# One-hots with nodes on partitions: compared from repeated rows of relative numbers in place of transposed, in the attention and the gate stage

## The chip, the cores and the metric

The kernel runs on one core of one Trainium2 chip. The metric is the device time of one execution in microseconds (us). Median before: 5861.45 us over 3 runs (5858.7 to 5862.68).

## What is computed

A graph network of four layers on 6250 nodes with 128 features and 100000 edges `(src, dst)`, sorted by `dst`. Each layer has a LayerNorm and a ReLU ahead of it and adds to `x`. Cut to what matters here:

```python
x = x + L0(h)                     # APPNP: two rounds of a normalised neighbour sum, then two dense layers
# L1, attention:
q, k, v = nodes @ Wq + bq, nodes @ Wk + bk, nodes @ Wv + bv
e = edge_attr_128 @ We
alpha = sum_per_head(q[dst] * (k[src] + e)) / sqrt(16)
attn = softmax of alpha over the edges of each dst
out = segment_sum(attn * (v[src] + e), dst)
x = x + L2(h)                     # two rounds of a neighbour mean, dense layers
# L3, gates:
xr, xc = h[src], h[dst]
gates = softmax(concat(x_src, x_dst, x_edge) @ W_gate + b_gate)   # three gates for each edge
out = segment_sum(gates[0] * x_src + gates[1] * x_dst + gates[2] * x_edge, dst)
```

## The kernel before, in words

Edges lie in tiles of 128, and nodes in 49 blocks of 128. A *step* is one tile of edges against one block of nodes (a tile that spans two blocks gives two steps): 832 steps. Four steps (`U = 4`) are a *part*, four parts (`PARTS = 4`) a turn; there are 208 parts. Buffers of a part are used in a ring of four, by `r = n % 4`; some PSUM banks and staging buffers in a ring of two (`RING2`). All order is written by hand: each engine runs its own list of steps, `edge_loop` and `stretch_loop` call the steps of an engine with a lag in parts, and semaphores join them.

`rel_col` holds, for each step and each edge on its partition, the edge's node relative to its block. A one-hot with **edges on partitions** is `iota == rel`, and is the weight of the product that adds messages to nodes (`hot`, `hot_sum`). A one-hot with **nodes on partitions** is needed to fetch a value of the destination node for each edge (`q[dst]` in the attention, the destination's logits in the gate stage) by a product with the block's rows. Before the change it is `hot` transposed: TensorE transposes, ScalarE copies PSUM to `hot_t`.

**Attention stage** (L1150 to L1470). Part `n` on each engine:
- GpSimd (`att_pool`, L1228): four indirect gathers of rows of `tab_kv` into `rows`, each followed by `weigh_part` (L1213), which multiplies the values of a part 39 parts back by their weights, or, as long as there is none, by a memset that paces the gathers (L1235). It may start part `n` once part `n - 4` is scored (`kv_done`).
- SyncE (`att_sp`): `att_load` (L1154), four loads of edge attributes for part `n`; `value_store` (L1171) of part `n - 3`, after its `kv_done`; `value_load` (L1166) of part `n - 37`, after the sums of four parts earlier (`win_done`). These stand in this order in one queue.
- VectorE (`att_dve`): `make_hot(n)` (L1417), then `score_part(n - 2)` (L1432, L1435, L1439, L1444), with the adds of summed messages (L1404) between.
- TensorE (`att_pe`): `turn(n)` transposes attributes (L1331) and `hot` (L1333); `products(n - 1)` gives `e` (L1344) and `q[dst]` (L1346); `sums` (L1357) of part `n - 40`.
- ScalarE: copies both transposes (L1275, L1276), weights and one-hots of the sums (L1248, L1253, L1258).

The 208 parts are cut into seven stretches; at the end of each, a chain for the softmax's maxima runs on VectorE, TensorE and ScalarE (`max_dve`, `max_pe`, `max_act`), and VectorE scores nothing meanwhile.

**Gate stage** (L1711 to L1800). GpSimd (`gathers`, L381) gathers rows of `tab_gate`, each gather followed by a memset (L384); part `n` waits for `gate_msg` of part `n - 4`. VectorE runs, for each part: `logits(n - 2)` (L1758 to L1763, waits for the gathered rows), `message(n - 3)` (L1781), `gates(n - 2)` (L1769 to L1773), `step_hot(n)` (L390), adds of part `n - 4` (L455). TensorE runs `logits(n - 1)` (L1743), `sums(n - 3)` (L432) and `turn(n)`, the transposes (L1732); ScalarE copies them (L1711), and does `exp` and `scale` (L1705, L1716). SyncE has nothing to do in this stage.

`d_reset` is a table in DRAM of one row of 128 for each step, written once in the set-up (L1915).

## Time and profile before

| | |
|---|---|
| median of 3 runs | 5861.45 us |
| the profiled execution | 5857.49 us, its span 5855.7 us |
| busy: PE, DVE, ACT, POOL | 68%, 51%, 24%, 59% of the span |
| attention stage, gathers from 1821.0 to 3200.1 us | about 1380 us |
| gate stage, gathers from 4590.3 to 5792.7 us | about 1204 us |
| granted TensorE clock over the span | 0.79 |
| DMA queue of SyncE (q1) | 611.37 MB, 32.6% of 16 engines |
| DMA queue of GpSimd (q0) | 224.30 MB, 14.1% of 16 engines |

PE is TensorE, PEld its weight loads, DVE VectorE, ACT ScalarE, POOL GpSimd, SPq the queue of SyncE, which issues most DMAs. "L381" is line 381 of the kernel. A busy share of the whole span mixes stages that have different limits, so stages are read one by one. Between the two stages here, and ahead of them, lie the set-up and four dense neighbour sums, which the change leaves as they are but for one store.

### The profile page before, as it was taken

To read this page: it belongs to the slowest core of one execution; us is meant where nothing else is said; L and a number is where in the kernel's file an instruction comes from. 1 tells how busy PE (TensorE), PEld (TensorE's weight loads), DVE (VectorE), ACT (ScalarE), POOL (GpSimd) and SP (SyncE) were. 2 spreads that over 40 slices of the span, in tenths; PEclk is the share of its full clock that TensorE was granted. 3 is DMA by queue.
4 is the path that set the end of the run, shared out by engine and by line. 5 is a ranking of instruction groups with operands and counts; after the bars stand their busy time and mean duration, and the time that the engine had idled before them with its cause. 6 is when DMAs were issued, how large, how long until landed. Compare 5 with 4: busy or idle time off the path is not lost.

```text
span 5855.7 us, 96074 instructions
## 1 busy us (share of the span) xinstructions
PE 3975.2 (68%) x24005; PEld 3106.2 (53%) x24006; DVE 2994.0 (51%) x9243; ACT 1419.4 (24%) x3648; POOL 3433.6 (59%) x4758
## 2 busy tenths in 40 slices
PE   1000586779996666666675619997998777777774
PEld 0000353446666566566565616665666766666664
DVE  7887510131135667667667652114113566666667
ACT  0012100010013144354443350002002333333333
POOL 7778988830005888888887320000000588888887
PEclk6555798989997798898898769999999655555555
DMA  9961343345545576576676206553552333333332
GB/s 370 368 223 43 120 146 101 124 141 192 192 132 165 168 216 192 180 216 192 183 214 185 71 15 193 189 174 106 191 192 89 97 92 92 92 92 92 92 92 76
DMA packets 537348, 892.81 MB, mean 152 GB/s; under 512 B 92522, under 2 KB 392140, under 8 KB 530910
## 3 DMA queue, kind: packets, MB, share of 16 engines
q1 hardware_dynamic: 420894, 611.37, 32.6%
q0 software_dynamic: 106912, 224.30, 14.1%
q10 hardware_dynamic: 9376, 55.32, 2.7%
q8 instruction: 56, 0.92, 0.1%
q14 instruction: 110, 0.90, 0.0%
HBM read 732.14 MB, written 158.57 MB: 152 GB/s over the span
## 4 chain that ended last, share of the span: by engine, by line
POOL 48%; PE 28%; issue 10%; DVE 7%; DMA 4%; ACT 1%; DVEq 1%; SPq 0%; ACTq 0%; POOLq 0%
PE ps L829 21%; POOL work L381 14%; POOL work L1228 11%; POOL d_adj L501 11%; POOL address L384 5%; POOL hw L1213 4%; PE ps L977 3%; POOL small L505 3%; DMA hw<-d_keys 1%; PE ps L836 1%; DMA d_adj<-logits,address 1%; DVE work L625 1%; PE ps L963 1%; POOL address L1235 1%; ACT work L941 1%
## 5 line engine op out<-in xcount | busy, mean ns | idle before, releaser
L381 POOL DMA_INDIRECT work<-tab_gate,src_col x832 | 797.9, 959 | 1275.9 <-DMA tab_gate<-logits 1141.4
L1228 POOL DMA_INDIRECT work<-tab_kv,src_col x832 | 838.4, 1008 | 748.8 <-DMA tab_kv<-hw 589.4
L829 PE MATMUL ps<-hw 128*128 128x384 bf16 x5096 | 876.1, 333 | 109.7 <-DMA hw<-d_adj 70.6
L829 PE MATMUL ps<-hw,work 128*128 128x384 bf16 x5096 | 866.7, 331 | 78.0 <-DMA work<-d_adj 78.0
L501 POOL DMA_INDIRECT d_adj<-logits,address x782 | 801.9, 1025 | 172.3 <-issue 163.8
L869 DVE TENSOR_TENSOR work<-work,ps 128x128 f32 (+1 forms) x208 | 59.8, 287 | 1487.6 <-ACT work L861 1473.6
L829 PEld LDWEIGHTS ps<-hw 128*128 128x128 bf16 x5096 | 504.9, 100 | 453.9 <-DMA hw<-d_adj 76.7
L829 PEld LDWEIGHTS ps<-hw,work 128*128 128x128 bf16 x5096 | 504.7, 99 | 413.1 <-issue 96.7
L861 ACT ACTIVATE work<-ps 128x128 f32 x208 | 57.6, 277 | 1847.2 <-PE ps L829 1847.2
L1743 PE MATMUL ps<-logits,work 128*128 x1664 | 343.9, 330 | 212.3 <-ACT work L1711 208.2
L1743 PEld LDWEIGHTS ps<-logits,work 128*128 128x128 f32 x1664 | 326.6, 292 | 294.4 <-issue 294.4
L432 PE MATMUL ps<-work 128*128 128x132 f32 x1664 | 395.9, 411 | 78.7 <-issue 69.6
L1213 POOL TENSOR_TENSOR hw<-hw 128x128 f32<-128x128 f32 (+1 forms) x712 | 356.8, 501 | 77.9 <-DMA hw<-d_value 65.6
L432 PEld LDWEIGHTS ps<-work 128*128 128x128 f32 x1664 | 341.6, 300 | 87.4 <-issue 85.6
L1357 PE MATMUL ps<-hw 128*128 128x136 f32 x1344 | 208.8, 302 | 216.2 <-POOL hw L1213 173.7
L1432 DVE TENSOR_TENSOR work<-ps,work 128x512 f32<-128x512 f32 x208 | 143.7, 691 | 413.4 <-DMA work<-tab_kv,src_col 232.8
L625 DVE SCALAR_TENSOR_TENSOR work<-hw,acc 128x256 bf16<-128x256 f32 x784 | 329.8, 486 | 47.6 <-DMA hw<-d_keys 39.4
L2042 PE MATMUL ps<-work 128*128 128x49 f32 x2 | 0.6, 415 | 490.7 <-DVE work L2139 490.7
L1716 ACT ACTIVATE work<-work 128x128 f32<-128x128 f32 x832 | 265.9, 390 | 275.3 <-DVE work L1773 275.3
L1357 PEld LDWEIGHTS ps<-hw 128*128 128x128 f32 x1344 | 181.1, 203 | 235.4 <-issue 234.9
L1275 ACT ACTIVATE work<-ps 128x512 f32<-128x512 f32 x208 | 124.2, 597 | 671.9 <-PE ps L1333 652.6
L384 POOL MEMSET address<- 128x256 int32 x832 | 273.6, 329 | 0.4
(403 smaller groups left out, 7026.7 us busy)
## 6 DMA issues: line engine op xcount, KB each, us to landing
hw<-d_adj SPq DMA_DIRECT2D x104, 800.0 KB
work<-d_adj SPq DMA_DIRECT2D x104, 800.0 KB
d_adj<-acc SPq DMA_DIRECT2D x52, 1568.0 KB, 21.3
hw<-d_adj SPq DMA_DIRECT2D x104, 768.0 KB
work<-d_adj SPq DMA_DIRECT2D x104, 768.0 KB
work<-attr_dram SPq DMA_DIRECT2D x832, 64.0 KB
d_value<-work SPq DMA_DIRECT2D x208, 256.0 KB
hw<-d_value SPq DMA_DIRECT2D x208, 256.0 KB
```

Of the source, the lines that this page charges most:

```text
L381: pool.indirect_dma_start(rows[:, r * U + u, 0:width], None, table, bass.IndirectOffsetOnAxis(sources[:, at:at + 1], 0)).then_inc(rows_in[ ...
L384: pool.memset(pause, 0).then_inc(sem("paced"), 1)
L432: nc.tensor.matmul(self.place(r, u), hot[:, r * U + u, :], message(r, u), start=True, stop=True).then_inc(sem("win_done"), 1)
L501: pool.indirect_dma_start(d_adj, bass.IndirectOffsetOnAxis(address[:, tile:tile + 1], 0), counts[:, tile:tile + 1], None).then_inc(adj_out ...
L505: pool.memset(early_pause, 0.0).then_inc(sem("paced"), 1)
L625: ins = nc.vector.scalar_tensor_tensor(same[:, k, :], key_rows[:, half, k // 2, :], key_col[:, at], weigh[:, k % 2, :], ALU.is_equal, ALU. ...
L829: last = nc.tensor.matmul(at, adj_half[2 * s + hf][:, k, :], xs[:, b, :], start=b == 0, stop=b == BLOCKS - 1)
L1213: ins = pool.tensor_tensor(at, at, wide.unsqueeze(3).broadcast_to((P, n, HEADS, HEAD_DIM)), ALU.mult)
L1228: pool.indirect_dma_start(rows[:, r * U + u, 0:KV], None, tab_kv, bass.IndirectOffsetOnAxis(src_col[:, at:at + 1], 0)).then_inc(rows_in[r] ...
L1357: nc.tensor.matmul(sum_place(6, u), hot_sum[:, r * U + u, :], msg_att[:, r * U + u, :], start=True, stop=True).then_inc(sem("win_done"), 1)
L1716: last = nc.scalar.activation(scaled[:, u, :], rows[:, r * U + u, D:KV], ACT.Copy, scale=msg_gate[:, r * U + u, GATE2:GATE2 + 1])
L1743: last = nc.tensor.matmul(banks(2 + r % RING2)[:, u * 4:u * 4 + 4], hot_t[:, r % RING2, u * P:(u + 1) * P], logits_dst[:, ds(blocks[u], 1) ...
```

## The change

In both stages the one-hot with nodes on partitions is no longer transposed. The relative numbers of all steps are written once to DRAM (`d_rel`), as `d_reset` was already; SyncE loads, for each part, its 4 x 128 numbers and repeats the row over all 128 partitions by the DMA (256 KB written for 2 KB of numbers), and VectorE compares it in place with the partition's number (`step_no[:, 0:1]`). TensorE's transposes of one-hots and ScalarE's copies of them are gone. In the attention the comparison replaces `make_hot`, in the gate stage it is added beside `step_hot`, which stays for the sums. PSUM banks and lags in the gate stage change with it.

```diff
+        d_rel = scratch("d_rel", (STEP_PAD, P))
+        att_node_hot = [part(hot_flat, r * U * P, (U * P,)) for r in range(PARTS)]
+        gate_node_hot = [part((attr_t_flat, hot_t_flat)[r // 2], r % 2 * U * P, (U * P,)) for r in range(PARTS)]
...
# att_load, behind the four attribute loads
+            wait(sp, sem("eq_done"), n - PARTS + 1)
+            sp.sem_inc(sem("turn"), 1)
+            rel_load(sp, att_node_hot[r], n, r)
+
+        def rel_load(sp, into, n, r):
+            sp.dma_start(into, d_rel[ds(n * U, U), :].rearrange("q e -> (q e)").partition_broadcast(P)).then_inc(rel_in[r], 16)
...
# att_act
-                nc.scalar.activation(hot_t[:, r % RING2], banks(1), ACT.Copy).then_inc(sem("att_copied"), 1)
...
# att_pe
             def turn(n, whole, r):
                 pe.wait_ge(attr_in[r], 16 * U * (whole + 1))
-                pe.wait_ge(sem("hot_ready"), ATT_HOT0 + n + 1)
...
-                for u in range(U):
-                    last = nc.tensor.transpose(banks(1)[:, u * P:(u + 1) * P], hot[:, r * U + u, :], ident[:])
...
             def products(n, r):
+                pe.wait_ge(sem("att_copied"), n + 1)
+                pe.wait_ge(sem("hot_ready"), ATT_HOT0 + n + 1)
...
# att_dve
-            def make_hot(n, r):
-                nc.vector.tensor_tensor(hot[:, r * U:(r + 1) * U, :], iota[:].unsqueeze(1).broadcast_to((P, U, P)),
-                                        rel_col[:, ds(n * U, U)].unsqueeze(2).broadcast_to((P, U, P)),
-                                        ALU.is_equal).then_inc(sem("hot_ready"), 1)
+            def make_hot(n, whole, r):
+                dve.wait_ge(rel_in[r], 16 * (whole + 1))
+                nc.vector.tensor_scalar(att_node_hot[r], att_node_hot[r], step_no[:, 0:1], None, ALU.is_equal).then_inc(sem("hot_ready"), 1)
...
+        def gate_sp(sp):
+            sp.wait_ge(sem("gate_zeroed"), 2 * GROUPS + 2)
+            def load(i, r):
+                n = i * PARTS + r
+                wait(sp, sem("gate_logits"), n - PARTS + 1)
+                sp.sem_inc(sem("turn"), 1)
+                rel_load(sp, gate_node_hot[r], n, r)
...
# gate_act
-            edge_loop(act, [(1, copy), (2, exp), (2, scale)])
+            edge_loop(act, [(0, exp), (0, scale)])
# gate_pe
-            edge_loop(pe, [(1, logits), (3, sums), (0, turn)])
+            edge_loop(pe, [(0, logits), (3, sums)])
# gate_dve
-            edge_loop(dve, [(2, logits), (3, message), (2, gates), (0, step_hot(hot_free)), (4, gate_sums.step_add(dve))])
+            def node_hot(i, r):
+                dve.wait_ge(rel_in[r], 16 * (GATE_TURN0 + i + 1))
+                nc.vector.tensor_scalar(gate_node_hot[r], gate_node_hot[r], step_no[:, 0:1], None, ALU.is_equal).then_inc(sem("node_hot_ready"), 1)
+            edge_loop(dve, [(2, logits), (3, message), (2, gates), (0, node_hot), (0, step_hot(hot_free)), (4, gate_sums.step_add(dve))])
...
# set-up, SyncE
+            sp.dma_start(d_rel.rearrange("(c p) e -> p c e", p=P), edge_f[REL]).then_inc(sem("reset_out"), 16)
```

Waits on `reset_out` ask for 32 in place of 16 (VectorE and ScalarE in the set-up and the attention's start, SyncE ahead of its first `att_load`). The gate's logits use a ring of four banks in place of two.

The order on SyncE in the attention's loop, before the change: L1154 loads attributes, L1171 stores values, L1166 loads values.

```order
L1166 DMA hw<-d_value 128x4x128
L362 ISA
L362 TENSOR_LOAD step_rows
L1154 ISA [waits att_turned]
L1154 DMA work<-attr_dram 128x128
```

And after the change, the end of the same turn: L1158 is the attribute load, L1165 the new load, L1183 and L1178 the store and the load of values.

```order
L1158 DMA work<-attr_dram 128x128
L1165 ISA [waits eq_done]
L1165 DMA work<-d_rel 128x512
L1182 REGISTER_ALU
L1183 ISA [waits kv_done]
L1183 DMA d_value<-work 128x512
L89 ISA
L1176 ISA [waits win_done]
```

The load of relative numbers stands behind the four attribute loads, and ahead of the store that waits for `kv_done`.

VectorE in the attention's loop after the change, around the comparison (L1427); L1452 ends the score of part `n - 3`, L1440 begins that of part `n - 2`.

```order
L1452 TENSOR_REDUCE hw<-work 128x4x8 [waits key_step]
L1413 ISA [waits win_added]
L1413 TENSOR_TENSOR acc<-acc,ps 128x136
L1427 TENSOR_SCALAR work<-work,step_no 128x512 [waits rel_in3]
L366 TENSOR_LOAD step_rows
L1440 TENSOR_TENSOR work<-ps,work 128x4x128 [waits rows_in1,value_out1,eq_done,win_done]
```

Where `make_hot` waited for nothing, the comparison waits for the DMA, and the score of a part stands behind it.

VectorE in the gate stage after the change, from the last operation of `gates` to the first of the adds.

```order
L1781 TENSOR_TENSOR work<-small 128x4x3 [waits gate_step]
L1804 TENSOR_SCALAR work<-work,step_no 128x512 [waits rel_in2]
L1798 REGISTER_ALU
L394 ISA [waits win_done]
L394 TENSOR_TENSOR work<-iota,rels 128x512
```

L1804 is new; L394 is L390 of before, and moves back by one operation.

## Rows read from the trace of the kernel before

**Rows 1.** Busy time by stretch: one of the attention, one of the gate stage.
```profile
core 0: us, PE busy (x) PEld busy (x) DVE busy (x) ACT busy (x) POOL busy (x), PEclk, DMA share, GB/s
...
2300.00:2500.00 200.00, 130.71 (x957) 122.84 (x956) 136.88 (x302) 88.18 (x236) 173.80 (x236) 0.88 0.65 194
...
4700.00:5000.00 300.00, 229.28 (x1040) 204.84 (x1040) 190.65 (x780) 108.33 (x312) 266.41 (x416) 0.57 0.34 92
```
**Rows 2.** Groups, gate stage: busy us, mean ns | idle before, releasers.
```profile
L381 POOL DMA_INDIRECT work<-tab_gate,src_col x832 | 797.9, 959 | 1275.9 <-DMA tab_gate<-logits 1141.4 <-issue 134.5
...
L384 POOL MEMSET address<- 128x256 int32 x832 | 273.6, 329 | 0.4
```
**Rows 3.** Groups of GpSimd in the attention, and lines with min/median/max ns.
```profile
L1228 POOL DMA_INDIRECT work<-tab_kv,src_col x832 | 838.4, 1008 | 748.8 <-DMA tab_kv<-hw 589.4 <-issue 131.2 <-DVE hw L1444 26.8
...
L1213 POOL TENSOR_TENSOR hw<-hw 128x128 f32<-128x128 f32 x672 | 313.5, 467 | 12.3
...
L1228 POOL DMA_INDIRECT work<-tab_kv,src_col x832: 942/989/2837, 1821.0 to 3200.1; - x167
...
L1213 POOL TENSOR_TENSOR hw<-hw x712: 408/413/2321, 2059.6 to 3308.9; 128x128 f32<-128x128 f32 x168, 128x512 f32<-128x512 f32 x10
```
**Rows 4.** Timeline, gate stage, one part: start us, us, instruction [idle before].
```profile
5003.02 0.17 DVE L1758 TENSOR_TENSOR small<-ps,work 128x16 f32<-128x16 f32 x1 [1.66 <-DMA work<-tab_gate,src_col]
...
5004.54 0.95 POOL L381 DMA_INDIRECT work<-tab_gate,src_col  x1 [0.16 <-issue]
...
5005.21 0.69 DVE L390 TENSOR_TENSOR work<-iota,rels 128x512 f32<-128x512 f32 x1
...
5005.49 0.33 POOL L384 MEMSET address<- 128x256 int32 x1
5005.98 0.95 POOL L381 DMA_INDIRECT work<-tab_gate,src_col  x1 [0.16 <-issue]
```
**Rows 5.** Line L2227, then timeline of the set-up: VectorE's one-input operations beside GpSimd.
```profile
L2227 DVE TENSOR_SCALAR t<-t x7: 626/626/627, 3966.0 to 3990.8; - x7
...
552.33 0.34 POOL L505 MEMSET small<- 128x256 bf16 x1
552.34 0.39 DVE L739 TENSOR_SCALAR work<-work,step_no 128x100 f32<-128x100 f32 x1
...
614.83 1.30 POOL L501 DMA_INDIRECT d_adj<-logits,address  x1 [0.17 <-issue]
...
615.13 0.88 DVE L2164 TENSOR_SCALAR acc<-acc 128x896 f32<-128x896 f32 x1
```
**Rows 6.** Timeline, attention: a gather beside the comparison of before.
```profile
2511.28 0.68 DVE L1417 TENSOR_TENSOR work<-iota,rels 128x512 f32<-128x512 f32 x1
...
2511.51 1.31 POOL L1228 DMA_INDIRECT work<-tab_kv,src_col  x1 [0.16 <-issue]
```
**Rows 7.** Timeline, attention, VectorE level with the gathers.
```profile
2568.64 1.89 SPq L1154 DMA_DIRECT2D work<-attr_dram  x4
...
2570.63 0.68 DVE L1417 TENSOR_TENSOR work<-iota,rels 128x512 f32<-128x512 f32 x1
...
2572.88 0.60 PE L1331 MATMUL ps<-ident,work 128*128 128x128 f32 x4
...
2573.95 0.69 DVE L1432 TENSOR_TENSOR work<-ps,work 128x512 f32<-128x512 f32 x1 [2.64 <-DMA work<-tab_kv,src_col]
...
2576.62 0.69 DVE L1444 TENSOR_REDUCE hw<-work 128x512 f32 x1 [0.17 <-issue]
```
**Rows 8.** Timeline, attention, VectorE behind the gathers, after a stretch's end.
```profile
2505.74 0.35 SPq L1171 DMA_DIRECT2D d_value<-work  x1
...
2509.06 1.89 SPq L1154 DMA_DIRECT2D work<-attr_dram  x4
...
2513.84 0.66 PE L1331 MATMUL ps<-ident,work 128*128 128x128 f32 x4 [1.14 <-DMA work<-attr_dram]
```
**Rows 9.** Timeline, a stretch's end: a scan of the maxima's chain, GpSimd's wait.
```profile
2237.35 1.79 POOL L1213 TENSOR_TENSOR hw<-hw 128x128 f32<-128x128 f32 x1
...
2255.56 1.40 POOL L1228 DMA_INDIRECT work<-tab_kv,src_col  x1 [5.49 <-DVE hw L1444]
```

45 lines of the change are left out of this document (20 added, 25 removed).

## The prediction

> **What bounds the kernel now.** I read the busy time by stretch first. In the gate stage GpSimd is busy 266 of 300 us and nobody else near it but TensorE, whose clock stands at 0.57, so close to its lower level of 1.2 GHz [rows 1]. The groups then show what GpSimd does there: gathers 797.9 us, pacing memsets 273.6 us, and 134.5 us of "issue" between them, together 1206 us, which is the whole stage (1204 us) [rows 2]. It waits for no other engine. VectorE waits 1.66 us of a part for the gathered rows [rows 4]. So each part lasts as long as four gathers with their memsets, 5.8 us, and the gate stage is GpSimd's own time.
>
> The attention is the same with a second load: gathers 838.4, issue 131.2, weighing 313.5 + 12.3 us, the rest memsets at its start. It waits 26.8 us for VectorE's last score operation L1444 [rows 3], in pieces of up to 5.5 us behind a stretch's end, when VectorE has been away for the maxima [rows 9]. Between the ends VectorE waits for the gathers (2.64 us of a part) [rows 7]. A part takes GpSimd 4 x (0.99 + 0.16 + 0.41) = 6.25 us by the medians [rows 3], 6.4 us with what holds it up, and 1380 / 208 = 6.6 us over the stage.
>
> Two things slow an instruction of GpSimd. In the attention a gather beside the comparison L1417, which reads two tensors in SBUF, takes 1.31 us where the median is 0.99: it ends 0.86 us behind L1417's end [rows 6]. And a product of GpSimd beside a long scan takes 1.79 us in place of 0.41 [rows 9]. GpSimd is the bound, so these count in full. **What the change does to GpSimd's own instructions is the question**, since TensorE and ScalarE, which it relieves, end no wait in either stage.
>
> **What is removed.** 832 transposes in each stage and 208 copies. In the attention and in the gate stage nothing of GpSimd's waits for them but through `kv_done` and `gate_msg`, and it waits for those 26.8 us and never [rows 2, 3]. I cost this at 0 to -10 us and take 0; the cover is the gather, and a part would have to be held by VectorE for it to count.
>
> **What is added for VectorE.** The new comparison has one input in SBUF. L2227, an operation of this kind over 896 elements, takes 0.626 us, less than L1417 with its two inputs for 512, 0.68 [rows 5, 6]. Two elements in a step, and the same step and fixed part for both, fit that: 512 steps in 0.68 and 448 in 0.626 give 0.84 ns a step and 0.25 us fixed, hence 256 steps in 0.47 us. With no fixed part at all it would be 0.626 x 512 / 896 = 0.36. I take 0.45 us, near the end that has a fixed part. In the attention that saves VectorE 0.23 us a part, in the gate stage it adds 0.45 us, where 1.66 us are idle: nothing on the path by itself.
>
> **What it does to GpSimd in the gate stage.** An operation of this kind and GpSimd hold each other up: L739, with the same operand `step_no`, takes 0.39 us for 100 elements and ends 0.06 us behind the memset that began with it, and L2164 takes 0.88 us where L2227, of its size, takes 0.63, while the gather beside it takes 1.30 us, and gathers otherwise 0.95 to 0.99 [rows 3 to 5]. Where VectorE waits, it costs nothing. Where GpSimd waits, all of it counts. L1804 begins where L390 begins now, at 5005.21, 0.67 us into a gather, and the memset wants to start at 5005.49 [rows 4]. Begun at once, L1804 ends at 5005.66 and the memset loses 0.17 us; begun when the gather lets go (0.25 us later, as L2164 did), the gather's end or the memset loses up to 0.4. I take 0.25 us for each of 208 parts: **+52 us**. Bounds: 0, if VectorE always is the one to wait; 208 x 0.45 = 94 us, if GpSimd loses the full length each time. The rows show that 0.3 us happen once in a gather, which is nearer to 0.25 than to either end.
>
> The Trainium skill's page "SBUF — State Buffer", section "Who interferes with whom", speaks against this edit: `tensor_scalar` can take both ports that VectorE shares with GpSimd, and then the other blocks fully, descriptor writing included, while an operation with two SBUF inputs only stops GpSimd's reads. Rows 5 and 6 agree that both happen, but not that a gather is stopped whole; by the rule taken at its word the sum would be the upper bound in both stages.
>
> **In the attention** the same operation takes the place of one that also cost something. By the difference of mean and median, gathers lose 832 x (1.008 - 0.989) = 16 us and products 672 x (0.467 - 0.413) = 36 us [rows 3]. Of these 52 us the maxima's scans take at six ends about 1.38 + 1.85 + 1.38 us (1.79 against 0.41 [rows 9]; the gathers' maximum 2.84 against 0.99 [rows 3]; the third taken like the first), 28 us. The 24 us left are L1417's. The new one is shorter but stops writes too; at 0.15 us a part, between nothing and the gate's 0.25, it costs 31 us: **+7 us** net. Bounds -24 (it holds nobody up) and 94 - 24 = +70.
>
> **The new wait.** `make_hot(n)` waited for nothing; now it waits for a DMA that SyncE issues behind the four attribute loads, and the score of part `n - 2` is queued behind it on VectorE, then `kv_done`, then SyncE's store, and at last GpSimd's gathers. At pace with the gathers: attribute loads are issued until 2570.53, and TensorE has them at 2572.88, 2.35 us later at the most [rows 7]; behind a stretch's end it is 2513.84 - 2510.95 = 2.9 us [rows 8]. The new load is issued 0.4 us later and moves 256 KB in place of 64, so I take 3.3 us: landing about 2574.2, the comparison done 2574.7, where the score began at 2573.95. VectorE falls 0.7 us further behind, at most 1.3. GpSimd has room for it within a stretch: it may start part `n` when `n - 4` is scored. At the stretches' ends the room is gone, as the 5.49 us show, and each of six costs 0.7 to 1.3 us more, 1.1 with the fuller DMA engines: **+7 us**, 0 to 30.
>
> Traffic: 208 x 256 KB = 53 MB more in each stage, 39 GB/s beside 194 in the attention and 44 beside 92 in the gate stage, with DMA shares of 0.65 and 0.34 [rows 1]. Transfers land later, which the ring of four covers: 0. In the gate stage the load of part `n` is issued once the logits of part `n - 4` are done, some 17 us ahead of its use, hidden. The one store of `d_rel` in the set-up lies beside the scatters of that time: 0.
>
> **The sum**: 52 + 7 + 7 = +66 us on the profiled execution's 5857.5 us gives **5923 us**; that execution stands 4 us below the median of the three runs. A difference of about 0.2%, 12 us, is what a measurement of this kernel can tell from no change.
>
> **The rivals.**
> 1. *The new wait becomes a loop that bounds the attention.* From one `kv_done` to the one of two parts later: store, value load and attribute loads take 3.3 us if the value load has not to wait, and 5.2 us as they do now behind an end (2505.74 to 2510.95) [rows 8]; then 0.4 for the issue, 2.9 to 3.9 for the landing, 0.45, and a score of 3.4 us (2573.95 to 2577.31) [rows 7]. That is 10.4 to 13.3 us for two parts, 5.2 to 6.7 for one, against GpSimd's 6.4. A stretch has 32 parts, and VectorE has to win back the slack that an end uses up: two of the ring's four parts, 12.8 us, since it scores two parts behind. Below 6.0 us a part it does; from 6.0 on it doesn't before the next end, and each end then costs GpSimd up to 12 us more: 5 x 12 = +60 on top, and at 6.7 another 0.3 x 208 = 62. Time 5980 to 6045. For it: SyncE is one queue and its DMAs come in bursts. Against it: TensorE no longer waits for VectorE in `turn`, so sums and value loads come sooner. A slower clock would feed it: TensorE's granted 0.88 in the attention [rows 1] might fall with the transposes gone.
> 2. *The one-input comparison doesn't hold GpSimd up* (it takes one port only, or VectorE always yields), and the 24 us of L1417 come back, with some of the 26.8 us wait, since VectorE has 0.23 us a part more. Faster: 5857 less 24 to 40, about 5827. It decides if GpSimd loses under 0.05 us a part in each stage. For it: half of L739's and L2164's delay fell on VectorE. Against it: the gather of 1.30 us.
> 3. *It all hides*: GpSimd loses as much in the gate stage as it gains in the attention, each some 10 to 20 us. 5850 to 5869.
>
> **How the numbers follow.** The forecast 0.56 (its own range 5880 to 5965), rival 1 0.16, rival 2 0.14, rival 3 0.14. The range takes in the forecast, rival 3, most of rival 2 and the near end of rival 1: 5825 to 5985. Faster by over 0.2%: rival 2 and a little of 3, 0.16. Within 0.2%: 0.12. Slower: 0.72.
>
> **What would show it.** In the gate stage, the memsets L384 or the gathers L381 with a mean above 329 and 959 ns, by together 0.25 us a part, or 60 ns an instruction pair; if both means stand and the stage still lasts 1204 us, the largest term is wrong. The new comparison at 0.45 us where nobody is in its way. In the attention, VectorE's wait ahead of the comparison, released by `d_rel`'s load, in place of the wait of L1432 for gathers; GpSimd's wait for the last score operation at 26.8 us plus some 7, and above 80 if rival 1 holds. Gathers and products of the attention with about the same means as now.

## The result, and the profile after

The changed kernel takes **6030.42 us** (4 runs, 6028.31 to 6033.04), the kernel before 5862.07 beside it (4 runs): ratio 1.0287, 95% interval 1.0269 to 1.0305. That is 168 us slower, where 66 were forecast. The profiled execution's span is 6026.5 us, 170.8 above the one of before.

The first question is where. GpSimd's gathers mark the stages (first and last start, by the lines' min/median/max rows):

| us | before | after | difference |
|---|---|---|---|
| ahead of the attention gathers | 1821.0 | 1825.2 | +4.2 |
| attention gathers | 1379.1 | 1489.5 | **+110.4** |
| from there to the gate gathers | 1390.2 | 1399.1 | +8.9 |
| gate gathers | 1202.4 | 1249.6 | **+47.2** |
| behind them | 63.0 | 63.1 | +0.1 |

Busy time by stretch, after, as [rows 1]:

```profile
core 0: us, PE busy (x) PEld busy (x) DVE busy (x) ACT busy (x) POOL busy (x), PEclk, DMA share, GB/s
2300.00:2500.00 200.00, 129.28 (x803) 118.89 (x803) 117.44 (x263) 70.23 (x196) 165.75 (x235) 0.85 0.77 232
4800.00:5100.00 300.00, 190.57 (x798) 175.48 (x798) 203.06 (x800) 74.67 (x250) 267.59 (x399) 0.50 0.46 132
```

In the gate stage GpSimd is as busy as before (267.6 of 300 us) but runs 399 instructions where it ran 416: each takes longer. In this window of the attention it runs 235 instructions in 165.8 us where it ran 236 in 173.8: each is shorter, and what the stage loses are waits, which the groups below show. TensorE is granted 0.50 in the gate stage, its 1.2 GHz level, where it was 0.57, with the transposes gone; GpSimd waits for no engine there.

The groups of after (as [rows 2, 3]: busy us, mean ns | idle before, releasers):

```profile
L385 POOL DMA_INDIRECT work<-tab_gate,src_col x832 | 812.8, 977 | 1276.9 <-DMA tab_gate<-logits 1141.9 <-issue 135.0
...
L388 POOL MEMSET address<- 128x256 int32 x832 | 305.8, 368 | 0.3
...
L1240 POOL DMA_INDIRECT work<-tab_kv,src_col x832 | 826.1, 993 | 902.8 <-DMA tab_kv<-hw 593.7 <-DVE hw L1452 180.8 <-issue 128.0
...
L1225 POOL TENSOR_TENSOR hw<-hw 128x128 f32<-128x128 f32 x672 | 284.5, 423 | 12.3
...
L1427 DVE TENSOR_SCALAR work<-work,step_no 128x512 f32<-128x512 f32 x208 | 122.0, 587 | 497.3 <-DMA work<-d_rel 497.0
```

Gate stage: the memsets' mean went from 329 to 368 ns and the gathers' from 959 to 977 [rows 2], 32.2 + 14.9 us, which is the stage's 47. Attention: gathers and products take 12.3 + 29.0 us *less* of GpSimd's time than before [rows 3], and the wait for the last score operation, L1452 (L1444 before), went from 26.8 to 180.8 us. VectorE in turn waits 497 us for the new load, in 185 of 208 parts. The waits of the attention that matter here (engine, line, waited for: us, times, longest):

```profile
DVE work L1427 <- DMA work<-d_rel: 497.0, 185, 9.9
...
PE ps L1366 <- DVE acc L1413: 194.8, 88, 4.6
POOL work L1240 <- DVE hw L1452: 180.8, 73, 21.9
```

And how they hang together, in the timeline of after (start us, us, instruction [idle before]); L1413 is VectorE's add of a sum, L1366 TensorE's sums, L1178 the value load, L1158 the attribute loads, L1165 the load of relative numbers, L1440 and L1452 a score's first and last operation:

```profile
2586.02 0.28 DVE L1413 TENSOR_TENSOR acc<-acc,ps 128x136 f32 x1
2586.45 1.17 PE L1366 MATMUL ps<-hw 128*128 128x136 f32 x8 [0.65 <-DVE acc L1413]
...
2588.03 0.38 SPq L1178 DMA_DIRECT2D hw<-d_value  x1
...
2589.33 1.89 SPq L1158 DMA_DIRECT2D work<-attr_dram  x4
...
2591.46 0.99 SPq L1165 DMA_DIRECT2D work<-d_rel  x1
...
2594.22 0.99 POOL L1240 DMA_INDIRECT work<-tab_kv,src_col  x1 [1.42 <-DVE hw L1452]
...
2596.30 0.70 DVE L1427 TENSOR_SCALAR work<-work,step_no 128x512 f32<-128x512 f32 x1 [2.16 <-DMA work<-d_rel]
...
2597.16 0.69 DVE L1440 TENSOR_TENSOR work<-ps,work 128x512 f32<-128x512 f32 x1 [0.16 <-issue]
...
2599.74 0.69 DVE L1452 TENSOR_REDUCE hw<-work 128x512 f32 x1
2600.34 0.28 DVE L1413 TENSOR_TENSOR acc<-acc,ps 128x136 f32 x1
```

Read it as a ring. VectorE's last add ends at 2586.30; TensorE's next sums wait for it; the value load waits for the sums; attribute loads and relative numbers stand behind the value load in SyncE's queue; the comparison waits for the relative numbers, the score is queued behind it on VectorE, and the score ends with the next last add, at 2600.62. 14.3 us for two parts, 7.15 a part; over the stage it is 1489.5 / 208 = 7.16. GpSimd needs 6.4. Before the change the same waits led from VectorE's adds to the attribute loads, but VectorE used what SyncE had just issued for part `n` only in the score of part `n`, two parts later, and `make_hot` waited for no transfer. Now the comparison of part `n`, which needs the newest load, stands ahead of the score of part `n - 2`.

### The profile page after: what moved, and what is told of

The parts are those of the page before. It is cut to its first block, busy times and chain, and to the rows that moved or that the text cites. A ratio compares the mean times of both kernels' runs of the same rounds, so it can differ in the third digit from the quotient of the medians.

```text
span 6026.5 us, 93729 instructions
## 1 busy us (share of the span) xinstructions
PE 3870.6 (64%) x22341; PEld 3007.3 (50%) x22342; DVE 3048.2 (51%) x9451; ACT 1195.4 (20%) x3232; POOL 3440.6 (57%) x4758
## 4 chain that ended last, share of the span: by engine, by line
POOL 44%; PE 29%; issue 12%; DVE 5%; DMA 5%; SPq 2%; ACT 1%; DVEq 1%; ACTq 0%; POOLq 0%
PE ps L833 21%; POOL work L385 13%; POOL d_adj L505 12%; POOL work L1240 7%; POOL address L388 5%; PE ps L981 3%; POOL small L509 3%; POOL hw L1225 2%; DMA work<-d_rel 2%; DMA d_adj<-logits,address 2%; PE ps L1366 1%; SPq L1158 1%; PE ps L840 1%; DVE acc L1413 1%; DMA work<-attr_dram 1%
## 5 line engine op out<-in xcount | busy, mean ns | idle before, releaser
L385 POOL DMA_INDIRECT work<-tab_gate,src_col x832 | 812.8, 977 | 1276.9 <-DMA tab_gate<-logits 1141.9
L1751 PE MATMUL ps<-logits,work 128*128 x1664 | 387.5, 356 | 465.5 <-DVE work L1804 465.5
L1751 PEld LDWEIGHTS ps<-logits,work 128*128 128x128 f32 x1664 | 370.4, 327 | 527.5 <-issue 527.5
L436 PE MATMUL ps<-work 128*128 128x132 f32 x1664 | 438.3, 445 | 6.6 <-DVE work L1789 5.6
L1366 PE MATMUL ps<-hw 128*128 128x136 f32 x1344 | 226.7, 319 | 301.5 <-DVE acc L1413 194.8
L436 PEld LDWEIGHTS ps<-work 128*128 128x128 f32 x1664 | 388.2, 336 | 7.4 <-issue 7.4
L1225 POOL TENSOR_TENSOR hw<-hw 128x128 f32<-128x128 f32 (+1 forms) x712 | 328.1, 461 | 85.0 <-DMA hw<-d_value 72.6
L1427 DVE TENSOR_SCALAR work<-work,step_no 128x512 f32<-128x512 f32 x208 | 122.0, 587 | 497.3 <-DMA work<-d_rel 497.0
L1366 PEld LDWEIGHTS ps<-hw 128*128 128x128 f32 x1344 | 193.4, 215 | 328.8 <-issue 328.3
L1353 PE MATMUL ps<-weights,work 128*128 128x128 f32 x1664 | 301.4, 340 | 24.7 <-issue 14.0
L388 POOL MEMSET address<- 128x256 int32 x832 | 305.8, 368 | 0.3
```

The costliest lines, as they stand in the source:

```text
L385: pool.indirect_dma_start(rows[:, r * U + u, 0:width], None, table, bass.IndirectOffsetOnAxis(sources[:, at:at + 1], 0)).then_inc(rows_in[ ...
L388: pool.memset(pause, 0).then_inc(sem("paced"), 1)
L436: nc.tensor.matmul(self.place(r, u), hot[:, r * U + u, :], message(r, u), start=True, stop=True).then_inc(sem("win_done"), 1)
L1225: ins = pool.tensor_tensor(at, at, wide.unsqueeze(3).broadcast_to((P, n, HEADS, HEAD_DIM)), ALU.mult)
L1353: nc.tensor.matmul(e[:, u * D:(u + 1) * D], attr_t[:, r % RING2, u * D:(u + 1) * D], weight("L1_We"), start=True, stop=True)
L1366: nc.tensor.matmul(sum_place(6, u), hot_sum[:, r * U + u, :], msg_att[:, r * U + u, :], start=True, stop=True).then_inc(sem("win_done"), 1)
```

## The experiments

All kernels run for this are built with one edit in common, to two wait counts that are loaded from memory, one in the set-up and one in the dense sums. They compute the same as without it.

```diff
                 need, = registers(ACTIVATION, zero_need_row, m, 1, ZERO_GROUPS)
+                need = smax(need, 1)
                 act.wait_ge(sem("zeroed"), need)
...
                     parts, = registers(SP, parts_row, v, 1, TILE_PARTS)
+                    parts = smax(parts, 1)
                     sp.wait_ge(sem("parts_landed"), parts)
```

They ran on four chips, A to D; which chip the first pair ran on is not on record. There the kernel before is itself slower: its medians were 6106, 6100, 6109 and 6259 us. So each kernel is set against the kernel before **of its own chip**, and read by stage. Chip A is that of the first experiment, B of the next four, C and D of the last two groups of four. Each row is one profiled execution; the same attention code gave 1398.4 and 1390.5 us on chip C and 1386.2 and 1393.1 on chip D, so I read nothing from differences below some 8 us in the attention. All stages in one table (gathers' and memsets' mean in ns, gate stage; "waits" is GpSimd's wait for VectorE in the gate stage):

| kernel | chip | ratio (95%) | ahead | attention | between | gate | gather, memset | waits |
|---|---|---|---|---|---|---|---|---|
| before | first | 1 | 1821.0 | 1379.1 | 1390.2 | 1202.4 | 959, 329 | 0 |
| changed | first | 1.0287 (1.0269 to 1.0305) | 1825.2 | 1489.5 | 1399.1 | 1249.6 | 977, 368 | 0 |
| load early | A | 0.9949 (0.9935 to 0.9964) | 1995.8 | 1385.6 | 1389.3 | 1248.9 | 976, 368 | 0 |
| changed + edit | B | 1.0171 (1.0150 to 1.0192) | 1987.7 | 1511.0 | 1397.3 | 1249.4 | 978, 367 | 0 |
| gate alone | B | 0.9986 (0.9973 to 1.0000) | 1987.5 | 1397.8 | 1391.7 | 1249.2 | 976, 368 | 0 |
| gate accumulating | B | 1.0019 (1.0006 to 1.0032) | 1976.7 | 1395.5 | 1390.5 | 1269.4 | 1039, 329 | 0 |
| early, both accumulating | B | 0.9947 (0.9927 to 0.9968) | 1992.3 | 1374.3 | 1386.4 | 1247.5 | 975, 329 | 31.4 |
| before + edit | C | 1.0017 (1.0002 to 1.0032) | 1996.5 | 1398.4 | 1390.8 | 1251.6 | 964, 329 | 48.8 |
| ScalarE for the gate | C | 0.9966 (0.9952 to 0.9980) | 1996.6 | 1377.5 | 1390.9 | 1263.1 | 972, 329 | 52.1 |
| gate accumulating, last | C | 0.9995 (0.9981 to 1.0009) | 1975.3 | 1390.5 | 1391.8 | 1248.0 | 975, 329 | 34.9 |
| load ahead of attributes | C | 1.0080 (1.0061 to 1.0099) | 1988.1 | 1453.3 | 1391.0 | 1251.3 | 979, 368 | 0 |
| before + edit | D | 1.0006 (0.9997 to 1.0014) | 2064.6 | 1414.8 | 1391.0 | 1330.4 | 969, 329 | 124.3 |
| changed + edit | D | 1.0104 (1.0088 to 1.0119) | 2063.1 | 1519.3 | 1395.9 | 1271.7 | 992, 335 | 35.0 |
| ScalarE for the gate | D | 0.9987 (0.9970 to 1.0003) | 2067.7 | 1386.2 | 1389.2 | 1369.3 | 961, 329 | 172.8 |
| early, accumulating, gate last | D | 0.9908 (0.9894 to 0.9923) | 2061.8 | 1393.1 | 1388.1 | 1293.1 | 982, 329 | 70.5 |

### The load issued early

```diff
         def att_load(sp, n, r):
...
-            wait(sp, sem("eq_done"), n - PARTS + 1)
-            sp.sem_inc(sem("turn"), 1)
-            rel_load(sp, att_node_hot[r], n, r)
...
                     value_store(sp, n, rn)
+                    if not isinstance(n, int) or n + PARTS < ALL_PARTS:
+                        sp.wait_ge(sem("eq_done"), n + 1)
+                        sp.sem_inc(sem("turn"), 1)
+                        rel_load(sp, att_node_hot[rn], n + PARTS, rn)
```

> The changed kernel, with the attention stage's loads of relative numbers issued some steps earlier: the load for part n+4 right behind the value store of part n, where its buffer has just been read, in place of behind the value load, the attribute loads and the wait for VectorE's comparison. The same bytes move and the same instructions run. Theory A (the new load closes a loop through SP's queue: adds -> sums -> value load -> attribute loads -> rel load -> comparison -> scores -> adds, 14.3 us for two parts, which is longer than GpSimd's own work): the comparison's wait for d_rel falls from 497 us to under 60, GpSimd's wait for the last score operation from 181 us to about 30, the attention gathers from 1490 to 1340 to 1380 us, and the total to 5890 to 5920 us, where the gate stage's loss is left. Theory B (the added transfers slow the other transfers and the gathers, whenever they are issued): the attention stage stays within 20 us of the changed kernel's, above 1465 us, and the total above 5990 us.

Theory A holds: attention gathers 1385.6 us, 6 above its range, where theory B asks for over 1465. Its rows (the gathers' waits, then the comparison's):

```profile
L1246 POOL DMA_INDIRECT work<-tab_kv,src_col x832: 947/990/2839, 1995.8 to 3381.4; - x167
...
  issue: 129.3, 804
  DVE hw L1458: 49.7, 14
...
L1433 DVE TENSOR_SCALAR work<-work,step_no x208: 475/491/1121, 1997.7 to 3375.1; 128x512 f32<-128x512 f32 x104
...
  DMA work<-d_rel: 58.3, 57
```

The comparison waits 58 us where it waited 497, and GpSimd 50 where it waited 181. The same bytes moved: traffic is not the cause, the place in SyncE's queue is. Nor is TensorE's clock: over the attention it is granted 0.83 here and 0.82 in the changed kernel of the first pair (0.87 before). The nearest attention stages as before are those of chips B and C, 1390.5 to 1398.4 us: with the load early, the change's attention part costs nothing. Also the 8.9 us between the stages are gone (1389.3). The total, forecast as 5890 to 5920, can't be compared: it came out on a chip where the kernel before took 6106.

### The changed kernel with the edit

> The changed kernel, computing the same, with one edit that all the experiment kernels carry: two wait counts that are loaded from memory in the set-up and the dense stage (ScalarE's wait on the zeroed groups, SyncE's wait on the landed parts) are first taken as the larger of the value and 1. If that edit costs nothing, the ratio to the kernel before is 1.0287 again, within 0.003, and the attention gathers run 1490 us and the gate gathers 1250 us from first to last. The run with the earlier loads ended 0.5% below the kernel before on its chip where its two stages together should have put it some 0.9% above, so the rival is that this edit shortens what lies ahead of the attention stage; then the ratio comes out below 1.02 with the same 1490 us and 1250 us.

The gate stage is as in the first pair (1249.4) and the attention's loss is there (1511.0), yet the ratio is 1.0171, as the rival in the forecast has it. What the edit is worth was left to a later run of the kernel before with it.

### The gate stage alone

The change's edits to `att_sp`, `att_act`, `att_pe` and `att_dve` are taken back; those to the gate stage stay.

```diff
-                nc.vector.tensor_scalar(att_node_hot[r], att_node_hot[r], step_no[:, 0:1], None, ALU.is_equal).then_inc(sem("hot_ready"), 1)
...
-            rel_load(sp, att_node_hot[r], n, r)
```

> The change in the gate stage alone; the attention stage transposes as before. Theory A (the two stages' losses are separate and add): gate gathers 1250 us from first to last, attention gathers 1380 us; the total lies 110 us below that of the changed kernel of the same chip. Theory B (the gate stage's extra 47 us come from what the attention stage leaves late): gate gathers about 1203 us, and the total 155 us below the changed kernel's.

Theory A: 1249.2 us in the gate stage whatever the attention is, 1397.8 in the attention (1380 forecast), and a median of 6089.4 us against the changed kernel's 6210.2, 121 us less (110 forecast). So on chip B the attention part of the change costs 1511.0 - 1397.8 = 113 us, and 6 between the stages.

### The accumulating comparison in the gate stage

```diff
-                nc.vector.tensor_scalar(gate_node_hot[r], gate_node_hot[r], step_no[:, 0:1], None, ALU.is_equal).then_inc(sem("node_hot_ready"), 1)
+                nc.vector.tensor_scalar(gate_node_hot[r], gate_node_hot[r], step_no[:, 0:1], 0.0, ALU.is_equal, ALU.add,
+                                        accum_out=run_col[:, r:r + 1]).then_inc(sem("node_hot_ready"), 1)
```

> As the kernel with the change in the gate stage alone, with the gate's comparison written with a second operation (add 0) and an accumulated output that nothing reads, so that VectorE does not pass two elements at a time and needs no second port; loads, waits and bytes are the same. Theory A (the gate stage loses its 47 us because the comparison in its two-at-a-time form takes SBUF's shared port from GpSimd): the comparison takes about 0.67 us or more, the memset's mean falls from 368 to about 330 ns and the gather's from 977 to about 960 ns, gate gathers 1202 to 1212 us, and the total 37 to 47 us below the kernel with the change in the gate stage alone. Theory B (the loads' traffic, 256 KB a part, slows the gathers): the means stay, and gate gathers stay near 1250 us.

Neither theory. The memsets were freed, as A said, but gathers grew from 976 to 1039 ns, and the stage to 1269.4 us. The timelines say why. First the gate stage alone, one part:

```profile
5303.62 0.64 DVE L1808 TENSOR_SCALAR work<-work,step_no 128x512 f32<-128x512 f32 x1
...
5304.01 0.49 POOL L389 MEMSET address<- 128x256 int32 x1
5304.18 0.67 DVE L395 TENSOR_TENSOR work<-iota,rels 128x512 f32<-128x512 f32 x1
...
5304.67 1.01 POOL L386 DMA_INDIRECT work<-tab_gate,src_col  x1 [0.16 <-issue]
```

and with the accumulating form:

```profile
5303.80 0.74 DVE L1808 TENSOR_SCALAR_CACHE_REDUCE work<-work,step_no 128x512 f32<-128x512 f32 x1
...
5304.22 0.33 POOL L389 MEMSET address<- 128x256 int32 x1
5304.46 0.08 DVE L1808 DVE_READ_ACCUMULATOR work<-work,step_no 128x1 f32 x1
5304.46 0.68 DVE L395 TENSOR_TENSOR work<-iota,rels 128x512 f32<-128x512 f32 x1
5304.70 1.27 POOL L386 DMA_INDIRECT work<-tab_gate,src_col  x1 [0.16 <-issue]
```

Beside the plain comparison the memset takes 0.49 us in place of 0.33, and beside the accumulating one 0.33. Count from the memset's start: with the plain form L395, the two-input comparison for edges, starts 0.17 us behind it and the next gather 0.66; with the accumulating form L395 starts 0.24 us behind it, as that comparison lasts 0.66 us (and 0.08 to read the accumulator), and the gather already 0.48, as the memset is no longer held. So the next gather begins 0.44 us before L395's end and takes 1.27 us; where it began 0.18 before the end, it took 1.01; where L390 ended ahead of it, in the kernel before, 0.95 [rows 4]. A gather that starts beside L395 is thus held until about 0.12 us before the end of L395. One that is under way when L390 starts isn't, and neither is a memset beside it (0.95 and 0.33 us in [rows 4]). The 80 ns a gather (1039 less 959) make 67 us, the whole loss of this version against 1202.4. In the plain form it is once a part 0.16 us for the memset and 0.06 for the gather, 46 us for 208 parts: the gathers' third of the stage's 47 us is L394's hold in the changed kernel, not that of the new comparison ahead of it.

The Trainium skill's page "SBUF — State Buffer", section "Who interferes with whom", says it this way: a VectorE operation with two inputs in SBUF stops what GpSimd reads and not what it only writes, a two-port form stops both, and `tensor_scalar` with an accumulated output has no such form. Both timelines agree on the memset in all three cases (0.33, 0.49 and 0.33 us). For the gather they agree only if it counts as reading: the section infers that descriptor generation is not stopped by `tensor_tensor`, and here the gather, a DMA of GpSimd, took 1.27 us beside one; the measurement decides.

### Early loads, both comparisons accumulating

The early load's edit, and the accumulating form at both comparisons.

> The changed kernel with the attention loads of relative numbers issued behind the value store (as in the run with the earlier loads, where the attention gathers ran 1386 us) and with both stages' comparisons in the accumulating form, whose output nothing reads. Theory A (loop and port explain all of the loss, and the attention stage now lacks the hold-up of the copy at line 1417 of the kernel before without another in its place): attention gathers 1350 to 1365 us, gate gathers 1202 to 1212 us, so 10 to 30 us under the kernel before in these two stages, and a total below it. Theory B (VectorE, with 0.2 us more a part in the comparison, becomes late in the attention stage): attention gathers above 1385 us with GpSimd's wait for the last score operation above 60 us.

Attention 1374.3 us, a little over A's 1350 to 1365 and 23.5 under the same chip's 1397.8; GpSimd's wait 52.5 us. GpSimd's own gathers (830.0 us) and products (336.7, 712 of them) sum to 1166.7 us, against 1196.7 (839.9 + 356.8) with the attention as before on the same chip, and 1178.7 (832.8 + 345.9) with the plain comparison early, on chip A: L1417 cost some 30 us, and the comparison that replaced it costs some 12, if the accumulating one holds nobody up. Over all profiles the sums are 1160 to 1167 with the accumulating one early and 1195 to 1203 as before, so both figures are good to some 10 us. The gate stage, forecast at 1202 to 1212, took 1247.5, with a new wait of 31.4 us for VectorE. Its gathers have a mean of 975 ns, not the 1039 of the run before, with the same order on VectorE and on the same chip; I come back to it at the version with the other order.

### The kernel before with the edit, chip C

> The kernel before, with the edit that all experiment kernels carry (two loaded wait counts taken as the larger of the value and 1). The changed kernel with this edit came to 1.0171 times the kernel before, where the changed kernel itself came to 1.0287. If the edit acts ahead of the attention stage alone, whatever follows it, this kernel comes to 0.985 to 0.992 times the kernel before, its gate gathers run 1203 us and its attention gathers 1380 to 1400 us. If the two ratios differ because the change costs less on these chips, it comes to 0.998 to 1.002.

1.0017 of the kernel before, so the edit costs nothing that counts (on chip D 1.0006), and the second reading holds: **the change costs less on these chips**, because the kernel before is itself slower there: in the gate stage, at 1251.6 us, it is no faster than the changed code (1251.3 us in the last run on this chip). Its memsets stand at 329 ns and its gathers at 964; 48.8 us are waits for VectorE that the first pair doesn't have.

### ScalarE makes the gate's one-hots

```diff
+            def node_hot(i, r):
+                n = i * PARTS + r
+                act.wait_ge(rel_in[r], 16 * (GATE_TURN0 + i + 1))
+                nc.scalar.activation(gate_node_hot[r], gate_node_hot[r], ACT.Abs, bias=step_no[:, 0:1], scale=-1.0).then_inc(sem("node_distance"), 1)
+                act.wait_ge(sem("node_distance"), n + 1)
+                act.sem_inc(sem("turn"), 1)
+                nc.scalar.activation(gate_node_hot[r], gate_node_hot[r], ACT.Relu, bias=1.0, scale=-1.0).then_inc(sem("node_hot_ready"), 1)
...
-            edge_loop(act, [(0, exp), (0, scale)])
+            edge_loop(act, [(0, node_hot), (2, exp), (2, scale)])
```

> Relative-number loads as in the changed kernel, issued early in the attention stage; the attention comparison in the accumulating form on VectorE, the gate's one-hots made by ScalarE in two passes, 1 less the distance of the relative number from the node's, cut at 0. Theory A (the gate stage loses its 47 us by what VectorE does more, the comparison and what it shifts; the 53 MB of loads cost nothing): the memset's mean is 329 ns, the gather's 959, gate gathers 1200 to 1208 us, attention gathers 1365 to 1380 us, and the total 15 to 30 us below the kernel before with the wait counts' edit, a version faster than both kernels. Theory B (the loads slow the gathers): the gather's mean stays at 970 or more and gate gathers above 1225 us.

Memset 329 ns and gather 972 (964 before on this chip): the 47 us shrink to 832 x 8 ns = 7. The same kernel on chip D has 961 ns where the kernel before has 969. With all 53 MB of loads in place and no comparison on VectorE, GpSimd's instructions are as fast as ever to within 8 ns: the loads don't lengthen them. Taken by their numbers, theory B's marks (970 ns or more, above 1225 us) are met on this chip, but the kernel before passes 1225 itself here (1251.6 us) and stands at 964 ns, so they don't tell the theories apart; chip D's 961 against 969 does. The forecast of the stage's time failed: 1263.1 us, 52.1 of them waits for VectorE. The total came out 27 us below the kernel before with the edit, where 15 to 30 were forecast.

### The accumulating comparison behind the two-input one

```diff
-            edge_loop(dve, [(2, logits), (3, message), (2, gates), (0, node_hot), (0, step_hot(hot_free)), (4, gate_sums.step_add(dve))])
+            edge_loop(dve, [(2, logits), (3, message), (2, gates), (0, step_hot(hot_free)), (0, node_hot), (4, gate_sums.step_add(dve))])
```

> As the kernel with the accumulating comparison in the gate stage alone, with that comparison issued behind VectorE's two-input comparison of edges in place of ahead of it. There one gather in four took 1.27 us, the one that began while the two-input comparison was running, 0.44 us before its end. Theory A (place matters: a gather that starts beside the two-input comparison is held until about its end): the two-input comparison starts 0.74 us earlier, beside a memset as in the kernel before, gathers go back to a mean of 959 to 965 ns, gate gathers 1200 to 1212 us. Theory B (the accumulating form itself lengthens the gathers): the mean stays near 1039 ns and gate gathers near 1269 us.

```profile
5304.39 0.69 DVE L395 TENSOR_TENSOR work<-iota,rels 128x512 f32<-128x512 f32 x1 [1.41 <-PE ps L437]
5304.51 0.33 POOL L389 MEMSET address<- 128x256 int32 x1
5304.99 0.95 POOL L386 DMA_INDIRECT work<-tab_gate,src_col  x1 [0.16 <-issue]
5305.00 0.74 DVE L1808 TENSOR_SCALAR_CACHE_REDUCE work<-work,step_no 128x512 f32<-128x512 f32 x1
```

L395 is beside the memset again, both it and the gather beside the accumulating comparison take their 0.33 and 0.95, and the gather's mean falls from 1039 to 975 ns (959 to 965 forecast): the accumulating form itself doesn't lengthen gathers, which excludes theory B. That the order on VectorE decides is not shown by it, though. The version with early loads had 975 ns in the old order, since L395 stood there 94 times, 187.6 us in all, for something that the profile calls "remote", and started beside a gather that was already under way:

```profile
5299.16 0.95 POOL L386 DMA_INDIRECT work<-tab_gate,src_col  x1 [0.16 <-issue]
...
5299.44 0.69 DVE L395 TENSOR_TENSOR work<-iota,rels 128x512 f32<-128x512 f32 x1 [0.57 <-remote]
```

What decides is what GpSimd starts while L395 runs; the order is one way to set that. The stage still took 1248.0 us, 34.9 of it waits for VectorE; in the kernel before on this chip they were 48.8.

### The load ahead of the attribute loads

```diff
+            wait(sp, sem("eq_done"), n - PARTS + 1)
+            sp.sem_inc(sem("turn"), 1)
+            rel_load(sp, att_node_hot[r], n, r)
             for u in range(U):
                 sp.dma_start(attr[:, r * U + u, :], a["attr"][ds(row0[u], P), :]).then_inc(attr_in[r], 16)
-            wait(sp, sem("eq_done"), n - PARTS + 1)
-            sp.sem_inc(sem("turn"), 1)
-            rel_load(sp, att_node_hot[r], n, r)
```

> The changed kernel with each part's load of relative numbers issued ahead of its four attribute loads in place of behind them, still behind the value load. Theory A (the loop runs over SyncE's queue, so each piece taken out of it shortens it): the four attribute issues, 1.9 us, leave a loop of 14.3 us for two parts, which makes 12.4 us or 6.2 a part, under GpSimd's own 6.4 to 6.6; attention gathers 1385 to 1430 us, GpSimd's wait for the last score operation 40 to 90 us. Theory B (the loads' landing alone is late, or the traffic): the wait for d_rel falls by less than a quarter of its 480 to 497 us and the attention gathers stay above 1470 us.

```profile
DVE work L1430 <- DMA work<-d_rel: 295.7, 165, 9.0
PE ps L1344 <- DMA work<-attr_dram: 286.1, 119, 11.4
...
POOL work L1243 <- DVE hw L1455: 137.6, 37, 20.5
```

Between the two: the attention's loss halves, from 105 to 113 us on chips D and B to 1453.3 - 1398.4 = 55, and the wait for `d_rel` falls by 40%. The direction is theory A's, its size isn't (1385 to 1430 forecast, and 40 to 90 us for GpSimd's wait, which is 137.6). Three comparisons in a row start at 2601.61, 2606.93 and 2614.97 us, 13.4 us for two parts where 12.4 were forecast: of the 1.9 us taken out, half comes back, and what is late next is the attributes (286 us, against 173 in the changed kernel). Moving the load by 2 us in the queue isn't enough; it has to leave the ring.

### The four on one chip, D

> The kernel before with the edit to two wait counts, again, as the yardstick by stage for the three kernels that run on the same chip. It should come to 1.000 to 1.003 times the kernel before. Theory A (chips differ in how late transfers land, and a late landing hides the port's price): where the part ahead of the attention gathers takes about 1820 us, the gate gathers take 1203 us, and where it takes about 1990, they take about 1250. Theory B (the two are unrelated): any other pair.

> The changed kernel with the same edit, against the kernel before of the same chip. Attention gathers 108 to 115 us longer. If transfers land as early there as in the first two profiles (1820 us ahead of the attention gathers), gate gathers 47 us longer and a ratio of 1.028; if they land late (1990 us), gate gathers within 5 us of the kernel before's and a ratio of 1.017 to 1.020.

> The kernel with the gate's one-hots on ScalarE, early attention loads and the accumulating comparison in the attention stage, again. Against the kernel before of the same chip: attention gathers 20 to 25 us shorter, gate gathers between 0 and 12 us longer, the memset's mean 329 ns, the total 8 to 25 us shorter (ratio 0.996 to 0.999). If the gate gathers are over 30 us longer, the loads themselves have a price.

> Early attention loads, accumulating comparisons in both stages, and the gate's placed behind the two-input comparison of edges. Attention gathers 20 to 25 us shorter than the kernel before's on the same chip, gate gathers 0 to 13 us longer, the memset's mean 329 ns and the gather's 965 to 976 ns, the total 8 to 25 us shorter, the same as with ScalarE within 10 us. If place does not matter, the gather's mean is near 1039 ns and the gate gathers 50 us or more longer.

Theory A of the first forecast paired 1820 us "ahead" with 1203 in the gate stage, and 1990 with 1250. Here it is 2064.6 and 1330.4, another pair, which by its words is theory B. The loss in the attention is 105 us (108 to 115 forecast) and the ratio 1.0104, below its 1.017 to 1.020, because the gate stage of the *changed* kernel is 58.7 us faster there: it waits 35 us for VectorE where the kernel before waits 124. What those waits are, in the kernel before on chip D:

```profile
4994.62 1.06 PE L1735 MATMUL ps<-ident,work 128*128 128x128 f32 x4
...
4998.22 0.60 ACT L1714 ACTIVATE work<-ps 128x512 f32<-128x512 f32 x1 [5.52 <-remote]
...
5003.98 0.95 POOL L382 DMA_INDIRECT work<-tab_gate,src_col  x1 [2.52 <-DVE work L1784]
```

The transposes end at 4995.68, and ScalarE's copy of them starts at 4998.22, 2.5 us later, released by "remote", which is nothing that the profile shows of this core. 68 times in 208 parts this wait stands there, 333.8 us together (the time in which the transposes were still running is in it), and here, 6 us later, GpSimd stands for 2.5. The change takes this copy out of the loop, and GpSimd's waits fall to 35 us. But the "remote" waits don't go with the copy. They stand at L395 on VectorE then, 149.2 us in the changed kernel, 96.9 in the last of the four, and most with ScalarE making the one-hots:

```profile
DVE work L395 <- remote: 489.7, 96, 10.1
```

So it isn't shown that the copy's removal is what the changed kernel gains here. With ScalarE making the one-hots the gate stage took 1369.3 us, forecast 0 to 12 us above the kernel before's 1330.4 and measured 38.9. By the mark set beforehand, over 30, the loads have a price. GpSimd's own instructions don't show one (gathers 961 ns against 969); the excess is its waits for VectorE, 172.8 us against 124.3, and whether the loads or ScalarE's two passes cause these no run tells apart. With the comparison on VectorE and the same loads they are 35.0 and 70.5, below the kernel before's, which speaks against the loads. The attention with ScalarE making the gate's one-hots is 28.6 us shorter than the kernel before's, a little more than forecast, and the total the same (0.9987, interval up to 1.0003), where 8 to 25 us were forecast.

The last kernel of the four, with early loads, both comparisons accumulating and the gate's behind L395, is the fastest of all: **0.9908 of the kernel before (0.9894 to 0.9923)**, attention 21.7 us shorter, gate stage 37.3 shorter, the median 55 us below where 8 to 25 were forecast, for the kernel before's waits there (124.3 us, against 70.5 in this one) are larger than I took them. The gather's mean of 982 ns lies above the forecast's 976. It beats both kernels on chip D. On a chip like the first it wasn't run. My estimate for there, from these rows: the attention gains about the same 20 us, while the gate stage, without waits to save, loses 0 to 16 ns a gather (975 less 959), up to 13 us.

## Why the prediction was wrong

The direction was right (0.72 on slower). The forecast of 5923 us missed 6030 by 107, and its range ended at 5985. Term by term:

**The gate stage, +52: right, measured +47.2.** 0.227 us a part in place of 0.25. The forecast named memset or gather as the one held up; it is the memset by two thirds (39 ns x 832 = 32.2 us, 18 ns x 832 = 14.9), and as forecast it goes both ways: L1804's median is 661 ns where it takes 479 undisturbed. The memset's part was tested by the form (329 ns with the accumulating one). The gathers' third is another thing than was forecast: L394, the two-input comparison that L1804 moves back, catches one gather a part and holds it for 0.06 us. That the total came within 5 us of the forecast is partly luck, since this was not in the sum. Its bounds were 0 and 94 us. What it didn't see is that a comparison which stops nobody can cost more than one that does, when the two-input operation behind it then runs beside the start of a gather: +67 us.

**L1417 gone, -24, and the new comparison, +31: net +7.** Measured where the ring isn't in the way: about -30 and +12, net -18 us, from three kernels on two chips; in the changed kernel itself gathers and products came to 41 us less. The size of the second was wrong: I took 0.15 us a part, and it was about 0.06.

**VectorE's new comparison, 0.45 us: right,** 477 to 492 ns when nobody is in its way.

**The new wait, +7 (0 to 30): this is the step that failed.** It was taken at +7 us and is behind the attention's +110.4 us and 8.9 more between the stages; with the load out of the ring both are gone (1385.6 and 1389.3 us). The working followed one part at pace, found VectorE 0.7 us further behind, and said that GpSimd "has room for it within a stretch". It didn't ask what the load's own issue waits for. It waits for VectorE: adds, sums, value load, then the queue. I had this ring as rival 1, and at a length of 10.4 to 13.3 us for two parts, and gave it 0.16. It is 14.3. The lower end let the value load go at once, 3.3 us from the store to the last attribute load. In the ring it never does: the sums wait for the last add, which comes only with the score's end, so that from add to last attribute load it is 4.9 us (2586.30 to 2591.22) every time round, close to the 5.2 of the upper end. Against that upper end two pieces were short. The landing: from the end of the attribute loads' issue to the comparison it was taken as 0.4 + 2.9 to 3.9 us, and it is 5.1 (2591.22 to 2596.30). And comparison with score: taken as 0.45 + 3.4 us, the last add ends 4.3 us behind the comparison's start (2596.30 to 2600.62). 4.9 + 5.1 + 4.3 = 14.3. Against the rival I had written that TensorE "no longer waits for VectorE" in `turn`, so that sums come sooner; TensorE in fact waits 194.8 us for VectorE's adds at L1366.

Rival 1's mechanism was right, and 5980 to 6045 held the result, but this is partly luck. Its price was worked out for 6.0 to 6.7 us a part; at 7.15 the same sum gives 5923 + 60 + 0.75 x 208 = 6139. What happened is plainer: the stage ran at the ring's pace, 7.16 in place of 6.63 us a part, 110 us. The slower clock that was named as feeding it didn't make the ring: granted 0.82 in the attention after (0.87 before), it was 0.83 with the load early and the loss gone. Its mark, GpSimd's wait above 80 us, was passed at 180.8. Rival 2 is excluded by the memsets' 368 ns, and by a kernel that is slower. Rival 3 fell with the gate stage.

**Traffic, 0: right.** The relative numbers' 53 MB a stage don't lengthen GpSimd's instructions: with them and without a comparison on VectorE the gathers' and memsets' means are those of the kernel before (961 to 972 and 329 ns, against 964 to 969 and 329 on the same chips). **The transposes' removal, 0: right for the first pair**, where the stages' losses are accounted for without it. On chip D the gate stage of the changed kernel is 58.7 us shorter than the kernel before's, and whether that is the copy's removal is open.

Open: what the "remote" waits are. The first pair has none of them, and they stand where the chips differ: ahead of the attention (348 us of them in the kernel before on chip C, 302 on D, and the part is 175 and 244 us longer there), in the attention (162 and 212), in the gate stage (245 and 380), and none between the two stages, where all chips agree. On chip B the three kernels with the plain comparison or the lone accumulating one have none in the gate stage, and the changed kernel's 1249 us are those of the first pair. Open too: the 4.2 us ahead of the attention, where the set-up's new store stands, which no run isolates; and how the fastest version does on a chip like the first.

## What to carry to other kernels

Before a load is put at the end of a queue, ask what the queue's earlier entries wait for, and follow that back: if it comes to the engine that will wait for the load, you have made a ring, and its length, not the latency, is the price. Issue the load where its buffer comes free, behind the last reader, if the ring of buffers allows it: the same bytes then cost nothing. And when VectorE and GpSimd share SBUF, count not only which operation stops GpSimd but what GpSimd starts beside its neighbour: a held memset cost 0.16 us, a held gather 0.32.

## What the runs showed of the hardware that was not expected

- A two-input comparison of VectorE (128x512) holds a gather that starts beside it until about 0.12 us before its end (gathers of 0.95, 1.01 and 1.27 us for starts 0.09, 0.18 and 0.44 us ahead of its end). It leaves a gather that is under way when it starts at 0.95 us, and a memset at 0.33. A one-input comparison holds the memset (0.49 us). The accumulating form holds neither (0.33 and 0.95 us), at 0.66 to 0.74 us in place of 0.48.
- A load of 256 KB, one row repeated over 128 partitions, landed 3.8 us after its issue in the median:

```profile
work<-d_rel SPq DMA_DIRECT2D x416, 256.0 KB, 3.8
```

- One program differs by up to 7% between chips (the kernel before: 5862, 6100 to 6109, and 6259 us; each chip was measured on one occasion, so chip and occasion aren't told apart), with nearly the same clock (0.78 to 0.79), and the difference sits in some stages only: against the first pair, on chips C and D 175 and 244 us ahead of the attention gathers, 19 and 36 in them, 49 and 128 in the gate gathers, none between the two (1390 to 1391). A change's ratio then depends on the chip: 1.029, 1.017 and 1.010 here.
